# At most two scatters of rows under way, and the first three experts' weights loaded behind most of them

## The reference

```python
scores = softmax(xt @ gate_w.T)              # 16 experts in 4 groups
# per row: the best 2 groups, the best 4 experts in them, their weights normed to 1
for e in range(16):
    a = swiglu(xt @ expert_up_w[e].T)         # up 512 -> 2*352, down 352 -> 512
    out = out + cw[:, e:e+1] * (a @ expert_down_w[e].T)
out = out + swiglu(xt @ shared_up_w.T) @ shared_down_w.T
```

## Time and profile before

| | |
|---|---|
| median of 3 runs | 1507.96 us (1506.36 to 1516.13) |
| the profiled execution's own time | 1507.08 us |
| its span | 1505.3 us |
| TensorE (matmul) busy | 1367.9 us, 91% |
| VectorE / ScalarE / GpSimd busy | 540.5 / 406.9 / 349.1 us |
| mean granted TensorE clock | 0.958 |

### The profile page before, as it was taken

The page is one execution under the profiler, slowest core; times in us unless marked ns, Lnnn a source line. Parts: engine busy times, 40 slices in busy tenths (PEclk is TensorE's granted clock), DMA queues, the critical chain, the costliest instruction groups (busy, mean ns, idle before and its releaser), DMA issues.

```text
span 1505.3 us, 26601 instructions
## 1 busy us (share of the span) xinstructions
PE 1367.9 (91%) x8703; PEld 861.6 (57%) x8704; DVE 540.5 (36%) x1125; ACT 406.9 (27%) x953; POOL 349.1 (23%) x423
## 2 busy tenths in 40 slices
PE   5966998999998899999349999999999999999997
PEld 4855776886777565544114445555555555555554
DVE  4786577559457226343001111111111111111111
ACT  3633544554343233120000001222221222222221
POOL 1301213333123123116720002222221122222222
PEclk9988999999896999999679999999999999999999
DMA  4673743653616411269620015556555555565430
GB/s 142 107 110 78 128 112 87 136 124 85 148 53 190 130 37 51 84 229 353 245 89 28 15 43 112 116 118 146 127 125 126 120 121 125 122 159 91 68 54 9
DMA packets 208338, 170.92 MB, mean 114 GB/s; under 512 B 71361, under 2 KB 160449, under 8 KB 208257
## 3 DMA queue, kind: packets, MB, share of 16 engines
q1 hardware_dynamic: 134880, 114.03, 28.6%
q0 software_dynamic: 16496, 34.23, 11.7%
q10 hardware_dynamic: 56880, 21.54, 6.8%
HBM read 90.93 MB, written 82.73 MB: 115 GB/s over the span
## 4 chain that ended last, share of the span: by engine, by line
PE 51%; another core or an unknown queue 5%; DVE 0%; issue 0%; POOL 0%; POOLq 0%; ACT 0%; DVEq 0%; ACTq 0%
PE pD L1861 14%; PE pG L1838 13%; PE pU L1852 12%; PE pD L1826 4%; PE pG L1815 3%; PE pU L1815 3%; PE pD L1847 2%; DVE front_region L1756 0%; POOLq L1604 0%; DVE xsT L1768 0%; POOL front_region L1657 0%; DVE acc_all L1762 0%; ACT y L1738 0%; ACT ups L1694 0%
## 5 line engine op out<-in xcount | busy, mean ns | idle before, releaser
L1676 POOL DMA_INDIRECT out<-y,ix x79 | 122.6, 1552 | 611.3 <-ACT y L1738 307.0
L1861 PE MATMUL pD<-w,aT 128*128 (+1 forms) x474 | 216.9, 593 | 1.2 <-ACT aT L1732 1.0
L1838 PE MATMUL pG<-w,xsT 128*128 x632 | 202.9, 464 | 3.2 <-issue 3.0
L1852 PE MATMUL pU<-w,xsT 128*128 x632 | 200.6, 460 | 0.0
L1838 PEld LDWEIGHTS pG<-w,xsT 128*128 128x128 f32 x632 | 120.0, 191 | 94.6 <-issue 44.4
L1790 DVE TENSOR_TENSOR a<-g,pU 128x352 f32<-128x352 f32 x79 | 41.2, 522 | 336.2 <-PE pU L1852 335.1
L805 PE MATMUL pProj<-front_region 128*128 128x256 f32 x624 | 160.6, 402 | 1.4 <-ACT front_region L609 0.7
L1108 DVE SCALAR_TENSOR_TENSOR front_region<-front_region,cw 128x256 f32<-128x256 f32 x288 | 134.8, 509 | 26.0 <-ACT front_region L623 22.6
L1861 PEld LDWEIGHTS pD<-w,aT 128*128 128x128 f32 (+1 forms) x474 | 89.8, 190 | 94.5 <-issue 79.0
L1852 PEld LDWEIGHTS pU<-w,xsT 128*128 128x128 f32 x632 | 114.4, 191 | 50.9 <-issue 1.0
L1738 ACT ACTIVATE y<-pD,wq 128x512 f32<-128x512 f32 x79 | 54.3, 687 | 306.1 <-PE pD L1861 271.7
(11 more groups left out here) (225 smaller groups left out, 1681.5 us busy)
## 6 DMA issues: line engine op xcount, KB each, us to landing
w<-in_up_T SPq DMA_DIRECT2D x16, 1408.0 KB
slot_rows<-zeros SPq DMA_DIRECT2D x79, 266.0 KB
xs<-slot_rows ACTq DMA_DIRECT2D x316, 64.0 KB
w<-in_down_T SPq DMA_DIRECT2D x16, 512.0 KB
front_region<-in_L_attn_hidden_states SPq DMA_DIRECT2D x16, 256.0 KB, 4.1
x2r<-in_L_attn_hidden_states SPq DMA_DIRECT2D x16, 256.0 KB, 4.2
partial_sums<-x2r SPq DMA_DIRECT2D x16, 256.0 KB, 2.5
x_normed<-x2n SPq DMA_DIRECT2D x16, 256.0 KB, 2.4
```

The lines of the kernel that those rows point to most:

```text
L1676: pool.indirect_dma_start(out=flat, out_offset=bass.IndirectOffsetOnAxis(ap=ix[1 - par][:, 0:1], axis=0), in_=y[1 - par][:, :], in_offset= ...
L1838: mm = pe.matmul(pG[0][:, 0:I], xsT[par][:, k, :], w[:, bass.ds(slot, 1), 2 * I * k:2 * I * k + I], start=(k == 0), stop=(k == DC - 1))
L1852: mm = pe.matmul(pU[0][:, 0:I], xsT[par][:, k, :], w[:, bass.ds(slot, 1), 2 * I * k + I:2 * I * (k + 1)], start=(k == 0), stop=(k == DC - 1))
L1861: mm = pe.matmul(pYq[:, :], aT[0:m, c, :], down[0:m, :, UPW + D * c:UPW + D * (c + 1)], start=(c == 0), stop=(c == 2))
```

## The change

Scatter `j` of a tile of rows uses the semaphore `s_scat[j % 2]`, and before it is issued GpSimd waits until all earlier scatters on that semaphore have landed, so that at most two are under way. The weights of experts 0, 1 and 2 leave their places in SyncE's stream; they are now issued between the first and the second store of `acc_all`, when 24, 28 and 32 scatters on `s_scat[1]` have landed (48, 56 and 64 in all), each load waited for before the next. ScalarE waits for both semaphores.

```diff
-            for s in range(2):
-                load_expert(sp, w[:, s], wup_d[s], wdn_d[s], s_w)
-                sp.wait_ge(s_w, 48 * (s + 1))
             sp.wait_ge(s_sup, 2 * UNITS)
             load_group(3)
-            sp.wait_ge(s_routed, 1)
-            load_expert(sp, w[:, 2], wup_d[2], wdn_d[2], s_w)
             ov = out.rearrange("b (t p) d -> p (b t) d", p=P)
             for gr in range(1, NG):
                 i = TPG * (gr - 1)
+                if gr == 2:
+                    for s in range(3):
+                        sp.wait_ge(s_scat[1], 16 * (24, 28, 32)[s])
+                        if s == 2:
+                            sp.wait_ge(s_routed, 1)
+                        load_expert(sp, w[:, s], wup_d[s], wdn_d[s], s_w)
+                        sp.wait_ge(s_w, 48 * (s + 1))
                 sp.wait_ge(s_sacc, TPG * (gr + 1))
                 sp.dma_start(ov[:, i + TPG:i + 2 * TPG, :], acc[:, i:i + TPG, :]).then_inc(s_base, 16)
...
             for i in range(NT):
                 for j in range(K):
+                    least(pool, s_scat[j % 2], 16 * ((K * i + j) // 2))
                     pool.indirect_dma_start(out=xs_d[:, :], out_offset=bass.IndirectOffsetOnAxis(
-                        ap=pos[:, i, j:j + 1], axis=0), in_=xall[:, i, :], in_offset=None).then_inc(s_scat, 16)
+                        ap=pos[:, i, j:j + 1], axis=0), in_=xall[:, i, :], in_offset=None).then_inc(s_scat[j % 2], 16)
...
-                    act.wait_ge(s_scat, 16 * NT * K)
+                    for i in range(2):
+                        act.wait_ge(s_scat[i], 16 * NT * K // 2)
```

More of the change, by code:

```diff
@@ L1556, in experts @@
         "xg_loaded", "gate_psum", "up_psum", "silu", "gated", "down_psum", "added"))
-    s_scat = sem("rows_scattered")
+    s_scat = [sem(f"rows_scattered{i}") for i in range(2)]
     s_xl, s_ml = [sem(f"slots_loaded{i}") for i in range(2)], [sem(f"slot_meta{i}") for i in range(2)]
```

## The result

The changed kernel takes 1457.88 us (median of 4 runs, 1451.04 to 1460.71), the kernel before 1509.39 (4 runs). The ratio is 0.966, with a 95% interval of 0.962 to 0.969: faster by 3.4%. The profiled execution has a span of 1449.3 us.

What follows compares the result with a forecast made beforehand. TensorE was taken to bound the kernel nearly everywhere, beside 5% of unexplained waiting. 1507.08 - 51.5 = 1455.6, plus 0.9 for the median, is 1456.5: forecast 1457 us, range 1452 to 1527.

Steps and rivals of the forecast that it cites:

- the pauses go: The author's own case, chance 0.50: TensorE's waits in the shared expert vanish, giving 1457 us, 1452 to 1466.
- The pauses (51.5 us): TensorE before units 14 and 15: 47.3 us idle plus 4.2 us of slow matmuls after, all saved.
- The case's cause: During GpSimd's scatters, late completion signals to other engines come from scatters with a backlog, not from DMA saturation alone.
- its own last sentence: Sign of a wrong prediction: late updates found while only two scatters are under way and no weights load.
- rival A: Lateness belongs to flowing scatters, not their backlog; TensorE waits until the later scatter end: 1525 us, slower, chance 0.24.
- Rival B: Late signals come from something other than DMA traffic; the 47.3 us stay: 1508 us, 1500 to 1515, chance 0.14.
- Rival C: Lateness returns with the moved weights from 756 us; partly faster, 1477 us, 1468 to 1487, chance 0.12.
- The interval of the scatters: GpSimd's pace with two under way: (2.5 + 0.3) / 2 = 1.4 us a scatter, instead of 1.27.
- The end of the scatters: The 48th scatter lands at about 756 us, the last at 788, 20 us before ScalarE's request at 807.5.
- The moved weights: Weights of experts 0, 1 and 2 all arrive before 835.6 us, so their new place in SyncE's stream costs nothing.

Runs made afterwards that it cites:

- 32 free scatters: Changed kernel with the limit of two under way for the first 32 scatters only, weights in their old place: 1470.73 us.

## Why the prediction was right, and where its reasons were not

*The forecast.* 1457 us against 1457.88 measured, for the case "the pauses go". That it fits within 1 us is partly luck: the kernel's own executions spread over 10 us.

*The pauses (51.5 us).* The term holds to the tenth: the stretch is 51.5 us shorter, 47.3 us of idle time and 4.2 of the half clock. The granted clock from 683 to 833 us is 1.00, where it was 0.61 in the first pause.

*The case's cause.* The prediction leaned on a backlog of scatters together with weights. That step failed. The limit alone gives everything and the move nothing; without weights, and with about two under way, the pauses stay; plain DMAs with some 27 under way make none. By its own last sentence, late updates with only two scatters under way and no weights loading, this step is refuted by the run with the moved weights alone. What survives is the reading that it names against rival A, an inflow slightly above what is drained: back to back at 1.27 us the pauses sum to 47 us, at 1.29 to 37 in the fastest execution, at 1.41 signals come up to 12.6 us late in the last third of the train and TensorE does not stop, at 1.50 there is nothing. The traces give the rate of the drain more closely than the author used it. In all six with 64 scatters that make TensorE pause (the kernel before, the moved weights alone, four under way, 1.29 us, aligned rows, half the bytes) the last late signals come 90.1 to 90.9 us after the first scatter, and with 32 free scatters 45.3 us after the first of them: each time 1.41 to 1.42 us a scatter, whatever the bytes. The prediction had the same figure in its hands, (64 x 1.27 + 8) / 64 = 1.40 us, and did not turn it into a threshold; that its forecast of 1.4 us for the limit lies on that very line was not seen, and the outcome owes something to luck.

*Rival A* had the cause more nearly right, lateness belongs to flowing scatters and not to their backlog, and drew the wrong result, because it took the lateness as given by their flowing at all. *Rival B*, and the rule of the Trainium skill beside it (page "SBUF — State Buffer", section "Who interferes with whom", DMA never contends with a compute engine), is answered: a change to the DMA issues alone took the lateness away. The rule stands for the matmuls, which never slowed, and says nothing of the signals after them. *Rival C* is refuted: with weights and scatters together at a DMA share of 0.70 from 763.6 to 799.5 us, no signal is late. Nor is one with the limit alone, where the share is 0.97 from 700 to 720 us; the scatters are further apart there still, 10 in 27 us.

*The interval of the scatters.* Mis-sized: 1.4 us forecast, 1.51 measured on the quiet stretch. A scatter's last packet is gone within 2.5 us of its issue, as the prediction took, but the scatter that waits for it starts 3.0 us after that issue (738.20 to 741.21, and 3.03 with one under way), not 2.8. By the Trainium skill's formula (page "DMA: Bandwidth & Descriptors", section "Anatomy of one DMA") 1.3 us was the estimate; the measurement is 0.2 us higher. That the miss did no harm is luck: it went to the right side of the line, and 1.3 us would lie on the wrong one.

*The end of the scatters.* 788 us forecast, last issue 797.07, landed at about 799.5. The margin before ScalarE's request was 5 us and not 20. From the first issue (683.18) to the 48th scatter's landing, when the first weights are issued at 763.60, it took 80.4 us and not 70.2: 5 us of that are the interval's, and the traffic of group 3 and the first store cost 80.4 - 48 x 1.51 = 8 us and not 3. From there to the last landing, with the loads, it took 36 us and not 31.6. The limit with the weights in their old place ends at 808.2 + 2.5 = 810.7, again 4 us before its request at 814.58. Both kernels stand close to the point at which scatters would be the bound; one under way is past it, by 65 us.

*The moved weights* cost nothing, as said, and bring nothing.

## What to carry to other kernels

When an engine waits although its releaser has long finished, and the trace says "remote" on one core, look at what issues something at a steady interval during that time, and vary that interval before varying volumes. Here a spacing without any wait for a landing did the same, so the plain way to state and to tune it is a distance between indirect DMAs. Take the time at which the lateness ends, too: divided by the number of DMAs issued it gives the distance to aim above. Test the parts of a change apart even when the whole does what was forecast: one of the two parts here brought nothing.

## What the runs showed of the hardware that was not expected

- Indirect DMAs of 128 rows issued by GpSimd 1.27 us apart make signals of engines' completions late; in the kernel before this begins between 15.7 and 20.8 us after the first of them. TensorE's come 2 to 50 us late there, and in one run GpSimd's own, which kept it idle by up to 1.5 us. Rows of half the length or another alignment change nothing, and plain DMAs every 0.54 us, from the same engine, do not do it. At 1.50 us apart there is nothing.
- The lateness ends as if each scatter took 1.41 to 1.42 us of something (90.1 to 90.9 us for 64, 45.3 for 32). At 1.41 us apart it is just there, up to 12.6 us for single signals, and costs 0.4 us of the stretch.
- Where the signals are held up is open. The runs speak against the DMA engines' load, the bytes, the count of completions and the number under way, and leave something that an indirect DMA of GpSimd has beyond a plain one; which part of it was not tested. Fewer rows in one scatter, which would tell rows from instructions, were not tried. Nor was the routed stage at a smaller distance, where its indirect DMAs come one in 7.6 us.
- A wait for a landing costs more than the packets show: 3.0 us from a scatter's issue to the start of the one that waits for it, where the last packet is gone within 2.5 us.
